# Second cross attention: probabilities turned in 32x32 blocks on VectorE, value products in 32x32 tiles of TensorE

## What is computed

```python
def _L1_xattn_ref(query, key, value, mask, w_q, b_q, w_k, b_k, w_v, b_v, w_o, b_o):
    Q = _split_heads(query @ w_q.T + b_q)      # 16 heads of 16
    K = _split_heads(key @ w_k.T + b_k)        # key = value = context, 257 rows
    V = _split_heads(value @ w_v.T + b_v)
    scores = jnp.einsum('bhqd,bhkd->bhqk', Q, K) * scale
    scores = jnp.where(mask, -jnp.inf, scores)
    probs = jax.nn.softmax(scores, axis=-1)
    attn = jnp.einsum('bhqk,bhkd->bhqd', probs, V)
    merged = attn.transpose(0, 2, 1, 3).reshape(b, s, h * dh)
    return merged @ w_o.T + b_o
```

## Time and profile before

| | us |
|---|---|
| median of 3 runs | 1003.32 (1000.01 to 1004.15) |
| the profiled execution | 999.8 |
| its span | 998.0 |
| TensorE busy | 906.3 (91%) |
| VectorE busy | 680.4 (68%) |
| ScalarE busy | 465.8 (47%) |
| GpSimd busy | 381.5 (38%) |
| the changed stage, first to last scores | 333.06 to 713.74 |

### The profile page before, as it was taken

The page is one execution under the profiler, slowest core; times in us unless marked ns, Lnnn a source line. Parts: engine busy times, 40 slices in busy tenths (PEclk is TensorE's granted clock), DMA queues, the critical chain, the costliest instruction groups (busy, mean ns, idle before and its releaser), DMA issues.

```text
span 998.0 us, 39451 instructions
## 1 busy us (share of the span) xinstructions
PE 906.3 (91%) x16050; PEld 741.3 (74%) x16050; DVE 680.4 (68%) x1765; ACT 465.8 (47%) x1197; POOL 381.5 (38%) x602
## 2 busy tenths in 40 slices
PE   4999889989746889999999999999977898999998
PEld 3777777777523678888888888888745568999976
DVE  5888798878775466666666666667568486555536
ACT  1222223322464645555555555556454434555541
POOL 6222223322396162333332242224047305766640
PEclk9999999999767999999999999999879799999999
DMA  7001400000001011111111111110037101222216
GB/s 254 25 19 56 155 4 4 5 4 4 3 1 48 3 50 51 51 50 54 62 66 65 52 50 51 50 50 3 2 132 307 43 0 59 81 75 77 79 65 237
DMA packets 29904, 60.96 MB, mean 61 GB/s; under 512 B 6000, under 2 KB 22480, under 8 KB 26416
## 3 DMA queue, kind: packets, MB, share of 16 engines
q1 hardware_dynamic: 25136, 48.00, 13.6%
q0 software_dynamic: 3744, 10.23, 3.0%
q10 hardware_dynamic: 864, 0.36, 0.2%
HBM read 49.27 MB, written 9.31 MB: 59 GB/s over the span
## 4 chain that ended last, share of the span: by engine, by line
PE 74%; issue 8%; DVE 7%; ACT 4%; POOL 4%; DMA 1%; DVEq 0%; ACTq 0%; POOLq 0%
PE psum L827 18%; PE psum L1605 7%; PE psum L903 7%; PE psum L261 6%; PE psum L234 4%; PE psum L890 3%; PE psum L1468 3%; PE psum L300 3%; PE psum L291 3%; PE psum L918 3%; PE psum L276 3%; ACT x_p L987 2%; PE psum L742 2%; PE psum L869 2%; PE psum L1488 1%
## 5 line engine op out<-in xcount | busy, mean ns | idle before, releaser
L987 ACT ACTIVATE x_p<-x_s,x_nmax 128x257 f32<-128x257 f32 x256 | 127.4, 500 | 100.0 <-DVE x_nmax L1020 99.9
L1051 DVE COPY x_pT<-psum 128x512 f32<-128x512 f32 x128 | 88.2, 689 | 56.3 <-PE psum L903 54.5
L1020 DVE CUSTOM_DVE_ANT_0 x_s<-psum,x_mask 128x257 f32<-128x257 f32 x256 | 94.3, 423 | 41.8 <-PE psum L890 41.1
L1076 POOL TENSOR_TENSOR x_ctx1l<-x_ctx,x_ctx1h 128x2064 fp32r<-128x2064 f32 x8 | 36.8, 4599 | 145.6 <-ACT x_ctx1h L770 145.6
L903 PE MATMUL psum<-ident,x_p 128*128 128x128 f32 x512 | 80.6, 280 | 5.6 <-ACT x_p L987 1.8
L1076 POOL TENSOR_TENSOR x_ctx0l<-x_ctx,x_ctx0h 128x2064 fp32r<-128x2064 f32 x7 | 32.2, 4599 | 104.1 <-ACT x_ctx0h L770 104.1
L903 PEld LDWEIGHTS psum<-ident,x_p 128*128 128x128 f32 x512 | 58.3, 141 | 17.1 <-ACT x_p L987 15.5
L918 PEld LDWEIGHTS psum<-x_v,x_pT 128*32 128x32 f32 x4096 | 48.3, 113 | 30.1 <-DVE x_pT L1051 18.2
L1708 POOL DMA_INDIRECT moe_outs<-me_out,me_goal x39 | 55.1, 1414 | 40.1 <-DVE me_out L1677 40.1
L1005 DVE TENSOR_SCALAR x_k<-psum,x_bk 128x258 f32<-128x258 f32 x128 | 57.7, 481 | 16.1 <-PE psum L827 16.1
L918 PE MATMUL psum<-x_v,x_pT 128*32 128x16 f32 x4096 | 61.0, 186 | 0.0
(11 more groups left out here) (293 smaller groups left out, 2744.3 us busy)
## 6 DMA issues: line engine op xcount, KB each, us to landing
x_ctx<-in_ctx SPq DMA_DIRECT2D x16, 1032.0 KB, 4.8
me_w<-in_moe_w SPq DMA_DIRECT2D x8, 1024.0 KB, 11.7
me_got<-moe_outs SPq DMA_DIRECT2D x8, 512.0 KB, 7.5
x_mask<-in_mask SPq DMA_DIRECT2D x16, 128.5 KB, 3.8
x<-in_x SPq DMA_DIRECT2D x4, 512.0 KB, 8.0
sm_cT<-in_ctx SPq DMA_DIRECT2D x16, 128.0 KB, 2.2
moe_rows<-me_xw SPq DMA_DIRECT2D x4, 512.0 KB, 4.9
me_ws<-in_moe_ws SPq DMA_DIRECT2D x1, 1024.0 KB, 4.8
```

The costliest lines, as they stand in the source:

```text
L987: nc.scalar.activation(x1_p[:, n, :], x1_s[:, rg, :], ACT.Exp, bias=x1_nmax[:, par, n:n + 1], scale=-1.0, accum_out=x1_sum[:, par, n:n + 1 ...
L1020: nc.vector.tensor_tensor_reduce(out=x1_s[:, rg, :], in0=psum[:, 2 + rg, 0:SK], in1=x1_mask[par][:, b, :], scale=1.0, scalar=-2 * MASKED, ...
L1051: nc.vector.tensor_copy(x1_pT[:, c].rearrange("p r k s -> p (r k s)"), psum[:, 6, :]).then_inc(x1["pT_ready"], 1)
L1076: eng.tensor_tensor(low[:], x1_ctx[:], high[:].bitcast(F32), ALU.subtract).then_inc(x1["ctx_split"], 1)
```

## The change

It does five things, all in the second cross attention:

- The turned values: `x1_values_turned` swaps the operands of the value projection, so that PSUM (bank 6, no longer used by the transposes) holds the values of batch b+1 with the channels on the partitions. Again 12 products, 256 moving columns. VectorE's 32x32 block transpose then writes `x_v` with keys on the partitions, in blocks of 32 (`take_values`).
- The probabilities are turned by two block transposes of 128x512 on VectorE, SBUF to SBUF, and no longer by 8 transposes on TensorE and two copies.
- The value products of a batch are one block, after the next batch's scores: for 4 groups, 8 blocks of 32 keys and 4 lanes a product of 32x32 weights and 16 columns, 128 products (256 instructions), each lane on its own diagonal tile.
- The keys are evicted with their bias by ScalarE, behind the exponentials, and ScalarE evicts no values.
- `plT` goes ahead of the scores in batch 0. The pieces in banks 0 and 1 no longer include the values. Before the mixer's table load ScalarE waits for the last `pT_ready`. The order of the value channels in the packed weights changes to suit.

```diff
@@ x1_tensor
-            def turn(t, b, c):
-                n = 2 * BT * t + 2 * b + c
-                pe.wait_ge(x1["exp_ready"], J * t + G * b + CB * (c + 1))
-                    pe.wait_ge(x1["pT_ready"], n)
-                for r in range(CB):
-                    for k in range(2):
-                        mm = nc.tensor.transpose(psum[:, 6, (2 * r + k) * P:(2 * r + k + 1) * P],
-                                                 x1_p[:, column(b, CB * c + r), k * P:(k + 1) * P], ident[:])
-                mm.then_inc(x1["pT_done"], 1)
...
+            def values(t, b):
+                i = BT * t + b
+                pe.wait_ge(x1["pT_ready"], 2 * (i + 1))
+                pe.wait_ge(x1["vT_free"], i + 1)
+                if b == 0 and t > 0:
+                    pe.wait_ge(x1["heads_ready"], t)
+                for rg in range(G):
                     n = column(b, rg)
-                    for k in range(2):
+                    c, r = rg // CB, rg % CB
+                    for kb in range(KB):
                         for j in range(L):
-                            mm = nc.tensor.matmul(psum[S * j:S * (j + 1), 7, n * DH:(n + 1) * DH], x1_pT[:, c, r, k, j * S:(j + 1) * S],
-                                                  x1_v[:, b % 2, k, (j * G + rg) * DH:(j * G + rg + 1) * DH],
-                                                  start=(b == 0 and rg == 0 and k == 0), stop=False, skip_group_check=True)
+                            own = slice(S * j, S * (j + 1))
+                            mm = nc.tensor.matmul(psum[own, 7, n * DH:(n + 1) * DH], x1_pT[own, b % 2, c, r, kb, :],
+                                                  x1_v[own, b % 2, c, kb, r * DH:(r + 1) * DH],
+                                                  start=(b == 0 and rg == 0 and kb == 0), stop=False, skip_group_check=True)
                 mm.then_inc(x1["pv_done"], 1)
...
+        def x1_values_turned(pe, n, ct):
+            b = n % BT
+            if n > 0:
+                pe.wait_ge(x1["vT_free"], n)
+            for m in range(KC):
+                for k in range(KC):
+                    mm = exact(psum[:, 6, m * D:(m + 1) * D], parts([w[:, k, m * P:(m + 1) * P] for w in x1_wvs],
+                                                                   [c[:, k, b * SP:b * SP + D] for c in ct]),
+                               k == 0, k == KC - 1, skip_group_check=True)
+            mm.then_inc(x1["vT_done"], 1)
...
             def tile(t, par, before, own, after):
                 for b in range(BT):
+                    here = own if b < BT - 1 else after
+                    if b == 0:
+                        piece(place("plT"), t, par, before)
                     if own:
                         scores(t, par, b)
-                    if b == 0:
-                        piece(0, t, par, before)
-                        if before:
-                            values(t - 1, BT - 1, 1)
-                    elif own:
-                        values(t, b - 1, 1)
-                    here = own if b < BT - 1 else after
+                    if b > 0 and own or b == 0 and before:
+                        values(t - (b == 0), (b - 1) % BT)
                     k = place("k0", (b + 1) % BT)
                     piece(k, t, par, here)
                     if b == 0 and before:
                         last_key(t)
                     piece(k + 1, t, par, here)
-                    if own:
-                        turn(t, b, 0)
-                    piece(k + 2, t, par, here)
+                    if here:
+                        x1_values_turned(pe, BT * t + b + 1, x1_cs[par if b < BT - 1 else 1 - par])
                     if b == 1:
                         piece(place("out"), t, par, before)
-                    if own:
-                        turn(t, b, 1)
-                        values(t, b, 0)
...
@@ x1_scalar
+            def take_keys(b, t):
+                for m in range(KC):
+                    n = place(f"k{m}", b)
+                    k_done(act, n, t)
+                    nc.scalar.activation(x1_k[:, b % 2, m, :], k_bank(n)[:, 0:SP], ACT.Identity,
+                                         bias=x1_bk[:, m:m + 1]).then_inc(x1[f"k{n % 2}_free"], 1)
...
+                    if own if b < BT - 1 else after:
+                        take_keys((b + 1) % BT, t)
...
-                    if own if b < BT - 1 else after:
-                        take_values(place("v", (b + 1) % BT), t)
...
@@ x1_vector
+            def take_values(t, b):
+                i = BT * t + b
+                dve.wait_ge(x1["vT_done"], i + 1)
+                if not (isinstance(i, int) and i < 2):
+                    dve.wait_ge(x1["pv_done"], i - 1)
+                nc.vector.transpose(x1_v[:, b % 2].rearrange("p c k r -> p (c k r)"), psum[:, 6, :]).then_inc(x1["vT_free"], 1)
+
+            def turn(t, b, c):
+                i = BT * t + b
+                n = column(b, CB * c)
+                hold(dve, x1["exp_ready"], J * t + G * b + CB * (c + 1))
+                if not (isinstance(i, int) and i < 2):
+                    dve.wait_ge(x1["pv_done"], i - 1)
+                nc.vector.transpose(x1_pT[:, b % 2, c].rearrange("p r k s -> p r (k s)"), x1_p[:, n:n + CB, 0:KB * S]).then_inc(x1["pT_ready"], 1)
...
-                    if own if b < BT - 1 else after:
-                        take_keys((b + 1) % BT, t)
+                    if own:
+                        turn(t, b, 0)
                     if b == 0 and before:
                         dve.wait_ge(x1["rinv_ready"], 2 * t)
...
+                    if b == 1 and before:
+                        n = place("out")
+                        k_done(dve, n, t)
+                        hold(dve, x1["x_biased"], t)
+                        row = x[:, bass.ds(t - 1, 1), :].rearrange("p o c -> p (o c)")
+                        nc.vector.tensor_tensor(row, k_bank(n)[:, 0:D], row, ALU.add).then_inc(x1[f"k{n % 2}_free"], 1)
+                    if own:
+                        turn(t, b, 1)
+                    if own if b < BT - 1 else after:
+                        take_values(t, b + 1)
...
@@ mix_scalar
             act.wait_ge(mx["weights_loaded"], 16 * 7)
+            act.wait_ge(x1["pT_ready"], 2 * BT * NT)
```

More of the change, by code:

```diff
@@ L842, in x1_piece @@
             kind, b, whose = PIECES[n]
[L843 to L846, removed]
+            k_free(pe, n, t)
+            if not there:
+                pe.sem_inc(x1[f"k{n % 2}_done"], 1)
+                pe.sem_inc(x1[f"k{n % 2}_free"], 1)
                 return
[L848 to L851, removed]
+            out = k_bank(n)
             if kind in ("k0", "k1"):
+                ct = x1_cs[(par + 1) % 2 if whose == 1 else par]
+                if kind == "k0" and b == 0:
+                    pe.wait_ge(x1["ctx_split"], t + 1 + 1)
                 m = slice(int(kind[1]) * P, int(kind[1]) * P + P)
@@ L856, in x1_piece @@
                                k == 0, k == KC - 1)
[L857 to L862, removed]
             elif kind == "plT":
+                pe.wait_ge(x1["exp_ready"], J * t)
                 low = LAST * ((t - 1) % U)
@@ L907, in values @@
-            def values(t, b, c):
-                pe.wait_ge(x1["pT_ready"], 2 * BT * t + 2 * b + c + 1)
-                if c == 0:
-                    kv_taken(pe, place("v", b), t - (b == 0))
-                    if b == 0 and not (isinstance(t, int) and t == 0):
-                        pe.wait_ge(x1["heads_ready"], t)
-                for r in range(CB):
-                    rg = CB * c + r
+            def values(t, b):
[5 more added lines that the diff above has]
+                for rg in range(G):
@@ L921, in values @@
                 mm.then_inc(x1["pv_done"], 1)
             def last_key(t):
-                kv_taken(pe, place("plT"), t)
+                k_taken(pe, place("plT"), t)
+                pe.wait_ge(x1["pv_done"], BT * t)
                 pe.wait_ge(x1["vlbd_ready"], (t - 1) // U + 1)
@@ L1037, in tile @@
                                                 x1_rinv[:].unsqueeze(2).broadcast_to([P, J, DH]), ALU.mult).then_inc(x1["heads_ready"], 1)
-                    for c in range(2):
-                        if b == 1 and c == 1 and before:
-                            n = place("out")
-                            kv_done(dve, n, t)
-                            hold(dve, x1["x_biased"], t)
-                            row = x[:, bass.ds(t - 1, 1), :].rearrange("p o c -> p (o c)")
-                            nc.vector.tensor_tensor(row, kv_bank(n)[:, 0:D], row, ALU.add).then_inc(x1[f"kv{n % 2}_free"], 1)
-                        if not own:
-                            continue
-                        n = 2 * BT * t + 2 * b + c
-                        dve.wait_ge(x1["pT_done"], n + 1)
-                        if not (isinstance(n, int) and n < 2):
-                            dve.wait_ge(x1["pv_done"], n - 1)
```

(6 more changed lines are left out.)

69 lines of the change are left out of this document (29 added, 40 removed), and 3 rows, old and new, of the table PIECES.

## The result

The changed kernel takes 1377.57 us (1373.23 to 1379.67, 4 runs) against 1003.74 us of the kernel before: ratio 1.373, 95% interval 1.3681 to 1.3778. The forecast was 1044, and the range ended at 1082. The direction was right and the size was not: +374 us where +40 stood.

A forecast was written before the change was run, and what follows sets the result against it. TensorE was taken to bound the stage, busy 24.78 of 25 us. Terms: 10.2 + 21.2 + 13.8 = 45.2, + 0.2 - 2.8 - 2.3 = +40.3 us, giving a median of 1044 us, range 1020 to 1082.

The forecast's parts named there:

- a block of 256 instructions at 2.28 us: New 32x32 value products on TensorE, per batch: 1.19 + 128 x 0.0085 us, priced from self attention's 8.5 ns pitch.
- a block of 256 instructions in self attention shows no gap: Prediction's argument from the earlier trace against the rival that the small products are dearer here.
- The rival of dearer products: Small value products cost 11.6 ns each instead of 8.9 with entry: +44 us, 1088 in all; chance 0.13.
- The clock stays at 1.00: Listed sign: TensorE's granted clock remains full in the changed stage.
- the prediction's remaining terms in the stage: Batch 0, 15 x 0.68 = 10.2 us; batches 1 to 3, 47 x 0.45 = 21.2; tile 1's wait gone, -2.8.
- VectorE's stall in batch 2: TensorE waits 0.92 us for VectorE's transpose before batch 1's value products, in 15 tiles: 13.8 us.
- ScalarE hidden: ScalarE's two key evictions of 258 columns, 0.4 us each, hide behind the value projection on TensorE.
- about 0.5 us per batch without that cover: Wait of the next scores for the last key's eviction if no value projection followed the keys.
- Start, tile 1, end: First scores at about 336.0, +0.2 us; tile 1's 2.82 us TensorE wait gone, -2.8; stage end shorter, -2.3.
- The 6.25 ns per instruction: Skill-page estimate for four tiles side by side, 1.6 us per block, change near zero; prediction used the trace's 8.5 ns.

The follow-up runs named there:

- Experiments 2, 4 and 5: 2: e_two (1310.39 us) and e_four (1298.26 us); 4: e_wide (1278.46 us); 5: b_more32b (1385.90 us).
- e_two: Changed kernel with the block of 128 value products issued in two halves, the second behind the first key piece, nothing left out: 1310.39 us.
- e_wide: Changed kernel with each small value product over 64 moving columns instead of 16, same number of instructions, sums not the reference's: 1278.46 us.
- e_four: Changed kernel with the value products issued in quarters of 32, spread over the whole step, nothing left out: 1298.26 us.
- e_half: Changed kernel with half of its small value products left out, 64 products per batch instead of 128: 1062.75 us.
- b_more: Kernel before with each half of its value products issued four times, copies into unused columns, 128 products of 128x32 per batch: 1328.19 us.
- b_more32b: b_more with its three copies as 32x32 products on the diagonal and one more wait before the last key's products: 1385.90 us.
- b_twice: Kernel before with each half of its value products issued twice, the copies into unused columns: 1043.03 us.
- e_quarter: Changed kernel with three quarters of its value products left out, 32 per batch as in the kernel before: 945.18 us, ratio 0.943.
- b_keys: Kernel before with only the evictions changed: ScalarE takes the keys behind the exponentials, VectorE copies the values: 1043.76 us, ratio 1.0417.

## Why the prediction was wrong

- **The step that failed is the largest term: a block of 256 instructions at 2.28 us.** The pitch was right (8.5 ns), and so were the count and what goes and stays. The block, though, was costed as if instructions were always there. They were not, and the trace of before shows it, in the very line of self attention that the pitch was taken from. The prediction held against its rival that "a block of 256 instructions in self attention shows no gap". That is true of the block in the earlier trace rows; but of the line's 32 blocks 12 are stopped in the middle, for 0.24 to 1.77 us and 6.8 us in all. Its group on the page of before, and two of the blocks:

```profile
L234 PE MATMUL psum<-sm_v,sm_pT 32*32 32x17 f32 x4096 | 42.6, 180 | 9.9 <-issue 6.8
...
123.59 1.21 PE L234 MATMUL psum<-sm_v,sm_pT 32*32 32x17 f32 x123
125.45 0.24 PE L234 MATMUL psum<-sm_v,sm_pT 32*32 32x17 f32 x5 [0.65 <-issue]
...
219.34 1.23 PE L234 MATMUL psum<-sm_v,sm_pT 32*32 32x17 f32 x124
222.34 0.24 PE L234 MATMUL psum<-sm_v,sm_pT 32*32 32x17 f32 x4 [1.77 <-issue]
```

  In the stage TensorE now waits 160.0 + 10.5 + 1.1 = 171.6 us for "issue".
- **The rival of dearer products had the mechanism and an eighth of the price.** It put 44 us on top of the forecast, and the measurement lies 334 above it. It named 34 KB of instructions in 2.2 us and a fetch of 0.98 us, and then took the fetch's transfer time for its cost. What the changed kernel shows are 80 stops of 2.1 us on average, and packets whose starts stand 3.3 us apart at the least, and some 3.4 to 4 us where they are wanted at once.
- **"The clock stays at 1.00" was the second failure, and costs about as much.** From first to last scores the stage took 748.1 us (336.1 to 1084.2) and before 380.7, so it grew by 367.4. 171.6 are gaps, 11.2 the waits in batch 2, and 28.6 the prediction's remaining terms in the stage (10.2 + 21.2 - 2.8). That leaves 156 us, an estimate by difference, for work done at half clock: the key and value products are then 0.21 apart, where it was 0.12, and scores take 1.10 us instead of 0.62. Experiments 2, 4 and 5 indicate that the length and tile of the products have their part in the clock: e_two and e_wide have the same 115 us of gaps in the stage and the same number of products, and a clock of 0.78 with 16 columns and of 0.98 with 64 (they differ in where the products stand, too).
- **The two failures together account for every version.** Take the stage's growth, less the version's own terms by the prediction's rows (an estimate), less its "issue"; what is left should be what half clock costs. Beside it stands (1 - granted clock) x stage, the time that the clock was short of in all. The own terms are the prediction's 40 for the new order, less 8.5 ns for each matmul left out, or with the 95 of e_wide, and 8.6 ns for each copy in the old order:

| version | stage grew by, us | own terms | "issue" | left | (1 - clock) x stage |
|---|---|---|---|---|---|
| changed | 367 | 40 | 172 | 156 | 202 |
| e_two | 300 | 40 | 115 | 144 | 150 |
| e_four | 287 | 40 | 41 | 206 | 187 |
| e_half | 54 | -30 | 47 | 37 | 39 |
| e_wide | 272 | 135 | 115 | 22 | 13 |
| b_more | 324 | 106 | 157 | 62 | 78 |
| b_more32b | 374 | 106 | 131 | 137 | 158 |
| b_twice | 47 | 35 | 16 | -4 | 9 |
| e_quarter | -60 | -64 | 3 | 1 | 0 |

  The two right-hand columns go together within some 20 us, but for the changed kernel, where a part of the half clock may fall into its longer gaps and cost nothing there (argued, not measured). No version in the table needs a third cause.
- **VectorE's stall in batch 2:** right. 0.76 us instead of 0.92 in 15 tiles, 11.2 us instead of 13.8.
- **ScalarE hidden:** right in the new order, as e_quarter shows; the two evictions take 0.48 and 0.47 us, 0.95 and not 0.8. The warning of "about 0.5 us per batch without that cover" came true in b_keys, at another place, 0.69.
- **Start, tile 1, end:** the stage starts 3.0 us later, as forecast (336.0). VectorE's 3.52 us in tile 1 doesn't show in front of TensorE, but in this kernel nothing can be read from that. The end went the other way: the gain of 2.3 us became a loss of 8, since the last blocks have their gaps too.
- **The 6.25 ns per instruction**, an estimate from the Trainium skill's overhead per matmul (TensorEngine Tiling (Array Packing), Instruction Overhead), was rightly left aside: the pitch measured in the block is 8.5. The Trainium skill's warning in the same section not to take the tiling factor from a small dimension is borne out, and by far more than the overhead that it names.

What is shown and what is open: that a gap is a wait for a packet of instructions is shown by its end, at one distance from a packet's end 568 times, and by the runs that changed the number and the spacing of the products. Whether the fetch could be made to run ahead is open, since no run here changed how instructions are fetched. And of the 156 us of half clock no run separates the part of the gaps from that of the tile.

No version here beats the kernel before with the whole work done. e_quarter's 945 us is what the rest of the change would bring if the value products needed no more instructions than now, but turned blocks of 32 keys leave only 32 rows to a product.

## What to carry to other kernels

Before tiling a product down, multiply out the instructions, weight loads included, and hold their number per microsecond against the densest stretch that the trace shows running without a gap, over the whole length of the stretch, not over a shorter one. Before taking a price from one clean block, read that line's whole group: an "issue" in its idle time is the warning, and here it stood on the page of before. If a rival's mechanism is sound but its price comes from one row of transfer time, price the latency as well, and what the clock does once TensorE stops. When an eviction moves to another engine, look at who wants the same bank next: it decided between nothing and 4%.

## What the runs showed of the hardware

- TensorE's instructions came in packets of 16 KB. One was used up by exactly 128 weight loads and 128 products where a block stopped twice (an x128 group stands between two gaps in the changed kernel and in e_wide). The small products that had run dry went on 1.2 to 1.6 us after a packet's end, 2.2 to 3.5 us after its start, in all eleven traces. Two packets never started less than 3.2 us apart in any trace, and dense demand got one per 3.4 to 4 us, some 64 to 75 instructions per microsecond on average. Of the 32 blocks of 256 instructions (weight loads counted) in self attention of the kernel before, 12 were stopped; of the 64 blocks of 512 in the changed kernel, all were.
- The granted clock doesn't follow TensorE's busy share. Between 400 and 700 us it was 0.77 at 90% busy (e_four, 32x32 products of 16 columns), 0.89 at 77% (b_more, 128x32) and 0.98 at 80% (e_wide, 32x32 products of 64 columns). More columns per product gave the faster kernel, by 99 us, at the same number of instructions (one run of e_wide).
